# Eight weight tiles of the second feed-forward stage: sign times coefficient on ScalarE, base matrix added by a transfer

## The chip, the cores and the metric

One core of a Trainium2 chip runs the whole program in one launch. The metric is the device time of one execution in microseconds. Before the change it is 2108.03 us, the median of three runs (2106.72 to 2109.63).

## The reference

A decoder block is computed for 2 x 512 tokens of width 1024, in fp32. It has three parts, each of them behind a layer norm and added to the residual `x`: a Mamba2 layer with its own gated MLP, a quantized attention-like product with a context, and a second gated feed-forward stage whose weights are "binary differences":

```python
def _binary_diff_weight(w, base):
    d = w - base
    coeff = jnp.mean(jnp.abs(d))
    return base + coeff * jnp.sign(d)

W1, W2, W3 = (_binary_diff_weight(w, mean_w) ...)      # 3584 x 1024 each
gate = jnp.einsum('bsh,ih->bsi', hidden_states, W1)
up   = jnp.einsum('bsh,ih->bsi', hidden_states, W3)
h = jax.nn.silu(gate) * up
return jnp.einsum('bsi,hi->bsh', h, W2)
```

The coefficient is a mean over a whole matrix, so no weight of the second stage can be formed before all of `w` and `base` has been read. The first stage of the kernel reads them in passing, keeps `sign(w - base)` as int8 in DRAM (`sign_spill`) and sums the absolute differences.

## The kernel before

**Stages.** The Mamba2 layer ends at about 445 us of the span. The first feed-forward stage (`m = 0`) runs to 1226.6 us. Then comes the context product, which has no weights of its own (1226 to 1293 us), and then the second feed-forward stage (`m = 1`) to the end.

**Products.** Each feed-forward product in fp32 is three passes over rounded high and low parts (hi x hi, hi x lo, lo x hi). `weight_hi` on ScalarE (L1360) rounds a weight tile of 128 x 512 into one of seven slots of `ring_hi`. `weight_lo` on VectorE (L1835) subtracts and writes `ring_lo`. TensorE waits for `ring_lo`, multiplies (L1030 for pair 0, L1086 for the pairs after it, L1134 for the down product) and frees the slot. The 28 row blocks of gate and up are taken as 14 pairs. Pair 0 is 16 plain steps of 12 matmuls (`plain`). Pairs 1 to 13 go by a seven-product scheme that first adds and subtracts weight quarters in place (`weight_sum`, L1812 to L1820).

**Forming a weight.** `form_weight(f)` on VectorE (L2010) does `sign * coef + base` on a tile of 128 x 1024, in place in the tile that holds the base. Numbers `f` = 0 to 3 are pair 0 and stand in `raw_even`. Numbers 4 to 7 are pair 1, in `raw_odd`. SyncE loads the base tiles (`load_second`, L702) and the int8 signs (`load_sign`, L709, four buffers). Of these, 0 and 1 are formed in the middle of the context product, 2 and 3 a little later, and 4 to 7 at steps 7 to 10 of the second stage.

**Order of the work.** There is no scheduler: each engine runs its list in the order in which it is written, and waits on semaphores stand between. Around the change the order is as follows.
- SyncE loads all 16 tiles of `q2` (the quantized context, L690), waits for TensorE's last product of the first stage, and loads base and sign tiles for pair 0. Later it stores the residual tiles (`x2_spill`, L728), and then loads pair 1 and its signs.
- VectorE ends the norm of the context product with `ctx_rsqrt(2)` and starts `ctx_round(0, range(0, 2))` (L2416, L2419). Then it adds the last down product to the residual (`down_out`, L1978), and goes on rounding.
- ScalarE's part of the rounding is a Relu (L1674) and the conversion to bf16 (L1677), element tile by element tile, between two VectorE steps.
- TensorE sums the columns of `q2` (L1153), waits for `down_out`, takes the mean of the residual (L1207, L1210), and runs the context product (`ctx_first`, L1167 and L1179).
- GpSimd issues the accumulating transfers that add the per-token means to `x2_spill` (L839, 16 of 256 KB), when the context product is over.

Of the kernel before, what the change touches and what calls it, by code (L numbers as in the profile page):

```python
# [157 lines left out]
N_FORM = len(FORM_NO)  # L158

# [28 lines left out]
def build(nc, x_t, ctx, w_mamba, w_dt, w_gu, w_dn, f_gu, f_dn, b_gu, b_dn, params, shapes_only,  # L188
# [243 lines left out]
    s_hs, s_hfree = sem("hs_ready"), sem("h_region_free")  # L432
# [14 lines left out]
    s_m1, s_m2, s_x2a = (sem(n) for n in ("first_mean_kept", "second_mean", "x2_mean_added"))  # L447
# [13 lines left out]
    s_sign, s_form = sem("sign_ready"), sem("second_formed")  # L461
    s_so = [sem(f"sign_stored{i}") for i in range(2)]
# [48 lines left out]
    def value_of(m, name):  # L511
        if name in ("b11", "t2"):
            return VA[m]
        return TLf[m][{"b21": 6, "t4": 6, "b22": 5, "b12": 4, "t3": 4, "t1": 3}[name]]

# [4 lines left out]
    def _(sp):  # L520
# [95 lines left out]
        def down_loads(m):  # L616

            if m == 0:
                sp.wait_ge(s_cd, CF_BLOCKS)
            else:  # L620
                sp.wait_ge(s_wlo, gw(1, PAIRS - 1, 6, 1) + 1)
                sp.wait_ge(s_x2a, 32 * KT)
# [65 lines left out]
        for i in range(CTX_TILES):  # L688
            sp.wait_ge(s_q2o, 16 * (i + 1))
            sp.dma_start(q2[:, i, :], q2_spill[i]).then_inc(s_q2[i // KT], 16)  # L690

        def load_second(p, x):
            if p > 2:
                sp.wait_ge(s_wlo, gw(1, p - 2, 6, x) + 1)
            elif p == 2:
                sp.wait_ge(s_wlo, fw(1, 7, x) + 1)
            elif p == 1:
                sp.wait_ge(s_tv, ALL_MADE[1])
                sp.wait_ge(s_x2, 32 * KT)
            else:  # L700
                sp.wait_ge(s_pd, W_END[0])
            sp.dma_start(rawF[p % 2][:, x, :, :], b_gu[p, x].rearrange("p (j h) -> p j h", j=4)).then_inc(s_rc[p % 2][x], 16)  # L702

        def load_sign(f):
            if f >= 4:
                sp.wait_ge(s_form, f - 3)
# [25 lines left out]
        load_second(1, 0)  # L732
        load_second(1, 1)
        for f in range(4, 8):
            load_sign(f)
# [26 lines left out]
    def _(pool):  # L762
# [19 lines left out]
        pool.wait_ge(s_hfree, 1)  # L782
# [16 lines left out]

        def store_down(f):  # L800
            pool.wait_ge(s_form, f + 1)
# [7 lines left out]
        for m in range(2):  # L809
# [23 lines left out]
            if m == 0:  # L833

                pool.wait_ge(s_x2, 32 * KT)
                for b in range(BATCH):
                    pool.wait_ge(s_m2, b + 1)
                    for o in range(KT):
                        pool.dma_start(x2_spill[o][:, HALF[b]], scr_c(7)[:, HALF[b]], accum_op=ALU.add).then_inc(s_x2a, 16)  # L839
# [435 lines left out]
    def _(act):  # L1275
# [86 lines left out]
        def inner_hi(w):  # L1362
# [25 lines left out]
            else:  # L1388
# [8 lines left out]
                if m == 1 and slot >= 5:  # L1397
                    act.wait_ge(s_form, N_FORM)
# [17 lines left out]
        def move_b22():  # L1416
            act.wait_ge(s_x2a, 32 * KT)
# [76 lines left out]

        def feed_forward(m):
            part_hi_of(m, "b12")
            for w in range(BASE_G[m], W_END[m]):
# [9 lines left out]
                if m == 0 and i - 1 in CTX_AT:  # L1507
                    q2_sum(CTX_AT[i - 1])
                if 1 <= i <= NP:
# [188 lines left out]
        ctx_round(0, range(KT + 2))  # L1698
# [32 lines left out]
    def _(dve):  # L1731
# [52 lines left out]
        def raw_in(m, p, x, j):  # L1784

            if m == 1:
                dve.wait_ge(s_form, FORM_NO["g", p, x, j // 2] + 1)
# [208 lines left out]
        def form_tile(f):  # L1996
            what = FORM_WHAT[f]
            if what[0] == "d":
                return stage_d[what[1] % 2][:, :]
            return rawF[what[1] % 2][:, what[2], 2 * what[3]:2 * what[3] + 2, :].rearrange("p a h -> p (a h)")  # L2000

        def form_weight(f):
# [4 lines left out]
            else:  # L2007
                dve.wait_ge(s_rc[what[1] % 2][what[2]], 16 * (PAIRS // 2 + what[1] // 2 + 1))
# [3 lines left out]
        def feed_forward(m):  # L2012
            make(m, "b12")
            for w in range(BASE_G[m], W_END[m]):
# [29 lines left out]
                if m == 1 and i in FORM_AT:  # L2044
# [231 lines left out]
        for q in range(NC):  # L2276
# [48 lines left out]
            elif h == BATCH - 1:  # L2325
                dve.sem_inc(s_hfree, 1)
# [131 lines left out]
        form_weight(0)  # L2458
        form_weight(1)
# [10 lines left out]
        form_weight(2)  # L2470
        form_weight(3)
# [80 lines left out]
```

## Time and profile before

| | |
|---|---|
| time, median of 3 runs | 2108.03 us (2106.72 to 2109.63) |
| span of the profiled execution, first to last instruction | 2105.5 us |
| TensorE busy | 2078.2 us (99%) |
| VectorE busy | 1679.2 us (80%) |
| ScalarE busy | 1056.9 us (50%) |
| chain that ended last | PE 87%, DVE 9%, ACT 2% |

The profile gives the profiled execution's span and no time of its own beside it. The median is 2.5 us above that span. PE is TensorE, PEld its weight loads, DVE VectorE, ACT ScalarE, POOL GpSimd, SP SyncE. A row in square brackets at the end of a timeline line tells how long the engine sat idle before it, and what released it. PEclk is the granted TensorE clock as a share of 2.4 GHz.

### The profile page before, as it was taken

How to read it: one execution, taken by the hardware profiler on the slowest of the kernel's cores; microseconds unless marked ns; L12 is line 12 of the kernel's file. 1: busy time of each engine (PE TensorE's matmuls, PEld its weight loads, DVE VectorE, ACT ScalarE, POOL GpSimd, SP SyncE). 2: the span in 40 equal slices, each digit the busy share in tenths (PEclk: the TensorE clock that was granted, in tenths of full speed). 3: DMA queues.
4: the chain of work that ended last, by engine and by line, in shares of the span. 5: the costliest groups of instructions: out<-in, count | busy, mean ns of one | idle time of the engine just before them, and what ended most of it. 6: DMA issues, size and time to landing. Idle time of an engine off the chain costs nothing.

```text
span 2105.5 us, 26520 instructions
## 1 busy us (share of the span) xinstructions
PE 2078.2 (99%) x9230; PEld 1669.2 (79%) x9234; DVE 1679.2 (80%) x2528; ACT 1056.9 (50%) x1748; POOL 185.3 (9%) x296
## 2 busy tenths in 40 slices
PE   8999999999999999999999999999999999999999
PEld 4777778788888888888888845788888888888887
DVE  8888686797777888888979899977677776698886
ACT  5333244457777787774444476533333333444442
POOL 0001101101111112110000002010000000100000
PEclk9999999999999999999999999999999999999999
DMA  3151116639889999896430045454444443846101
GB/s 136 40 203 57 51 61 200 145 117 325 292 294 339 325 349 346 294 347 255 148 133 1 1 180 123 163 197 145 174 146 174 159 150 123 323 175 205 55 21 60
DMA packets 136434, 370.07 MB, mean 176 GB/s; under 512 B 16688, under 2 KB 27568, under 8 KB 132656
## 3 DMA queue, kind: packets, MB, share of 16 engines
q1 hardware_dynamic: 110640, 287.12, 39.6%
q0 software_dynamic: 25088, 80.23, 11.3%
q8 instruction: 74, 1.21, 0.2%
q10 hardware_dynamic: 576, 1.05, 0.1%
q14 instruction: 56, 0.46, 0.1%
HBM read 288.12 MB, written 84.41 MB: 177 GB/s over the span
## 4 chain that ended last, share of the span: by engine, by line
PE 87%; DVE 9%; ACT 2%; issue 1%; DMA 1%; ACTq 0%; SPq 0%; DVEq 0%
PE pair L1086 47%; PE pair L1134 24%; PE pair L856 7%; PE pair L1030 2%; DVE conv_out L2172 2%; PE pair L849 1%; PE pair L1096 1%; DVE weights_lo L1737 1%; PE pair L968 1%; PE pair L989 1%; DMA sign_in_ab<-sign_spill 1%; PE pair L1167 1%; PE pair L995 0%; DVE centred L2383 0%; DVE hs L2091 0%
## 5 line engine op out<-in xcount | busy, mean ns | idle before, releaser
L1086 PE MATMUL pair<-comb_hi,ring_hi 128*128 128x512 f32 x1456 | 566.5, 389 | 0.0
L1086 PE MATMUL pair<-comb_lo,ring_hi 128*128 128x512 f32 x1456 | 566.4, 389 | 0.0
L1086 PE MATMUL pair<-comb_hi,ring_lo 128*128 128x512 f32 x1456 | 566.4, 389 | 0.0
L1134 PE MATMUL pair<-inner_ring_a,ring_hi 128*128 128x512 f32 x1080 | 332.5, 389 | 0.0
L1086 PEld LDWEIGHTS pair<-comb_hi,ring_hi 128*128 128x128 f32 x1456 | 273.3, 188 | 57.2 <-issue 0.4
L1086 PEld LDWEIGHTS pair<-comb_hi,ring_lo 128*128 128x128 f32 x1456 | 273.3, 188 | 56.7
L1086 PEld LDWEIGHTS pair<-comb_lo,ring_hi 128*128 128x128 f32 x1456 | 273.3, 188 | 56.6
L1134 PEld LDWEIGHTS pair<-inner_ring_a,ring_hi 128*128 128x128 f32 x1080 | 202.6, 188 | 42.0
L1134 PE MATMUL pair<-inner_ring_a,ring_lo 128*128 128x512 f32 x540 | 210.1, 389 | 0.0
L1360 ACT ACTIVATE ring_hi<-ring_sum 128x512 fp32r<-128x512 f32 x160 | 100.5, 631 | 147.8 <-DVE ring_sum L1820 145.7
L1835 DVE TENSOR_TENSOR ring_lo<-raw_a,ring_hi 128x512 fp32r<-128x512 f32 x146 | 99.6, 688 | 53.4 <-ACT ring_hi L1360 51.6
L1134 PE MATMUL pair<-inner_ring_b,ring_hi 128*128 128x512 f32 x432 | 133.4, 390 | 0.0
L1134 PEld LDWEIGHTS pair<-inner_ring_a,ring_lo 128*128 128x128 f32 x540 | 101.3, 188 | 21.1
L1835 DVE TENSOR_TENSOR ring_lo<-ring_sum,ring_hi 128x512 fp32r<-128x512 f32 x160 | 109.7, 686 | 9.9 <-ACT ring_hi L1360 7.8
L856 PE MATMUL pair<-act_hi,weights_hi 128*128 128x512 f32 x256 | 108.5, 424 | 1.7 <-DVE act_lo L2274 1.4
L1986 DVE TENSOR_TENSOR pair<-coeff_in 128x1024 f32<-128x1024 f32 x84 | 103.1, 1227 | 0.0
L856 PE MATMUL pair<-act_hi,weights_lo 128*128 128x512 f32 x256 | 99.9, 390 | 0.0
L856 PE MATMUL pair<-act_lo,weights_hi 128*128 128x512 f32 x256 | 99.8, 390 | 0.0
L1486 ACT ACTIVATE sign_out<-pair 128x1024 int8<-128x1024 f32 x84 | 85.2, 1014 | 23.8 <-DVE pair L1986 23.8
L1134 PEld LDWEIGHTS pair<-inner_ring_b,ring_hi 128*128 128x128 f32 x432 | 81.1, 188 | 17.3 <-issue 0.5
L1360 ACT ACTIVATE ring_hi<-comb_hi_f 128x512 fp32r<-128x512 f32 x72 | 45.3, 630 | 94.6 <-PE pair L1134 48.5
L1360 ACT ACTIVATE ring_hi<-raw_a 128x512 fp32r<-128x512 f32 x146 | 87.4, 624 | 10.6 <-DVE raw_a L1815 7.0
(397 smaller groups left out, 3610.0 us busy)
## 6 DMA issues: line engine op xcount, KB each, us to landing
coeff_in<-f_gu SPq DMA_DIRECT2D x56, 512.0 KB, 5.3
coeff_in<-b_gu SPq DMA_DIRECT2D x56, 512.0 KB, 6.9
weights_raw<-w_mamba SPq DMA_DIRECT2D x44, 512.0 KB, 3.5
raw_a<-w_gu SPq DMA_DIRECT2D x28, 512.0 KB, 6.3
raw_a<-w_gu SPq DMA_DIRECT2D x56, 256.0 KB, 6.2
u_spill<-gate_a POOLq DMA_DIRECT2D x56, 256.0 KB, 4.9
coeff_in<-f_dn SPq DMA_DIRECT2D x28, 512.0 KB, 4.7
coeff_in<-b_dn SPq DMA_DIRECT2D x28, 512.0 KB, 6.6
```

The lines of the kernel that those rows point to most:

```text
L849: ins = pe.matmul(out[:, HALF[half]], w[:, wi, k * P:(k + 1) * P], a(half, k), start=k == 0 and n == 0, stop=k == KT - 1 and n == 2)
L856: ins = pe.matmul(out, w[:, wi, k * P:(k + 1) * P], a(b, k), start=k == 0 and n == 0, stop=k == KT - 1 and n == 2, skip_group_check=True)
L968: pe.matmul(ps[2][:, g * 512:(g + 1) * 512], bx_cur[:, 2 + g, :], xbc[:, 4 + g * HPG:4 + (g + 1) * HPG, b * SEQ + c * P:b * SEQ + (c + 1) ...
L989: ins = pe.matmul(ps[2][:, hd * P:(hd + 1) * P], x_dt[:, hd, :], att[:, hd, :], start=True, stop=c == 0)
L1030: ins = pe.matmul(out, wt[:, slot, col], a, start=j % 2 == 0 and kk == 0 and n == 0, stop=j % 2 == 1 and kk == KH - 1 and n == 2, skip_gro ...
L1086: ins = pe.matmul(out, wt[:, slot, col], a, start=t in (0, 1, 3) and kk == 0 and n == 0, stop=kk == KH - 1 and n == 2, skip_group_check=True)
L1134: ins = pe.matmul(out, wt[:, slot, col], a, start=t in (0, 1, 3) and k == 0 and n == 0, stop=k == SC_PAIRS - 1 and n == 2, skip_group_chec ...
L1360: act.activation(WRH[:, slot, :], src, ACT.Copy).then_inc(s_whi, 1)
L1486: act.activation(sign_out[:, c % 2, :], dif_ps[:, :], ACT.Sign).then_inc(s_sign, 1)
L1835: TT(WRL[:, slot, :], src, WRH[:, slot, :].bitcast(F32), ALU.subtract).then_inc(s_wlo, 1)
L1986: TT(dif_ps[:, :], dif[:, c % 2, 0, :], dif[:, c % 2, 1, :], ALU.subtract).then_inc(s_cd, 1)
L2172: ins = STT(tile[:, :, back:], src[:, :, :SEQ - back], conv_par[:, s, TAPS - 1 - back:TAPS - back], tile[:, :, back:], ALU.mult, ALU.add)
```

## The change

The weights with `f` = 0 to 7 are no longer formed on VectorE. ScalarE writes `sign * coef` into the place of the weight (`scale_sign`), and GpSimd then issues a transfer that adds the base matrix from DRAM into that place (`add_base`). SyncE no longer loads the base of pairs 0 and 1. The weights from `f` = 8 on are formed as before. One semaphore, `s_added`, now counts the base adds and the mean adds of `x2_spill` together.

```diff
+SCALED = 8
+SCALE_AT = {5: 4, 6: 5, 7: 6, 8: 7}
+ADDED = (16 * 4, 16 * (SCALED + BATCH * KT))
+MEANS_ADDED = 16 * (4 + BATCH * KT)
...
@@ sync
+        load_q2(0)
...
         for i in range(2):
             sp.wait_ge(s_so[i], 16 * (CF_BLOCKS // 2))
-        load_second(0, 0)
+        sp.wait_ge(s_pd, W_END[0])
         for f in range(4):
             load_sign(f)
-        load_second(0, 1)
+        load_q2(1)
+        for f in range(4, 8):
+            load_sign(f)
         load_down(0)
         load_down(1)
...
         spill_x2(1)
-        load_second(1, 0)
-        load_second(1, 1)
-        for f in range(4, 8):
-            load_sign(f)
@@ gpsimd
-        pool.wait_ge(s_hfree, 1)
+        pool.wait_ge(s_yt, NC + 1)
...
+        def add_base(f):
+            pool.wait_ge(s_scaled, f + 1)
+            _, p, x, h = FORM_WHAT[f]
+            pool.dma_start(form_tile(f), b_gu[p, x, :, h * BLK:(h + 1) * BLK], accum_op=ALU.add).then_inc(s_added, 16)
...
             if m == 0:
+                for f in range(4):
+                    add_base(f)
+                pool.wait_ge(s_added, ADDED[0])
                 pool.wait_ge(s_x2, 32 * KT)
...
+                pool.wait_ge(s_added, MEANS_ADDED)
+                for f in range(4, SCALED):
+                    add_base(f)
@@ scalar and vector, raw_in
-            if m == 1:
-                act.wait_ge(s_form, FORM_NO["g", p, x, j // 2] + 1)
+            if m == 1 and p < 2:
+                act.wait_ge(s_added, ADDED[p])
+            elif m == 1:
+                act.wait_ge(s_form, FORM_NO["g", p, x, j // 2] - SCALED + 1)
@@ scalar
+        def scale_sign(f):
+            act.wait_ge(s_sgn[f % 4], 16 * (f // 4 + 1))
+            if f == 0:
+                act.wait_ge(s_mc, 1)
+                act.wait_ge(s_pd, W_END[0])
+            elif f == 4:
+                act.wait_ge(s_tv, ALL_MADE[1])
+                act.wait_ge(s_x2, 32 * KT)
+            kind = FORM_WHAT[f][2]
+            act.activation(form_tile(f), sign_in[f % 4], ACT.Copy, scale=coef[:, kind:kind + 1]).then_inc(s_scaled, 1)
...
         ctx_root(2, bank(1))
-        ctx_round(0, range(KT + 2))
+        for f in range(2):
+            scale_sign(f)
+        ctx_round(0, range(2))
+        scale_sign(2)
+        ctx_round(0, range(2, KT + 2))
+        scale_sign(3)
         centred_squares(1)
@@ vector
-        form_weight(0)
-        form_weight(1)
...
-        form_weight(2)
-        form_weight(3)
...
-                if m == 1 and i in FORM_AT:
+                if m == 1 and i in FORM_AT and FORM_AT[i] >= SCALED:
                     form_weight(FORM_AT[i])
```

On ScalarE, where the context product starts (L1668 and L1704 are the end of `ctx_root(2)`, L1674 and L1710 the Relu of the rounding, L1677 and L1713 the conversion), the order before is:

```order
845 L1668 ACTIVATE scratch_c_166<-scratch_c_166 128x512
846 L1674 ACTIVATE scratch_c_165<-scratch_c_165,params 128x512 x3
847 L1677 ACTIVATE q_0_162<-scratch_c_165,quant_columns 128x512
848 L1674 ACTIVATE scratch_c_165<-scratch_c_165,params 128x512
849 L1677 ACTIVATE q_0_162<-scratch_c_165,quant_columns 128x512
```

and in the changed kernel:

```order
845 L1704 ACTIVATE scratch_c_166<-scratch_c_166 128x512
846 L1527 ACTIVATE raw_even<-sign_in_ab,coeff 128x1024 x2
847 L1710 ACTIVATE scratch_c_165<-scratch_c_165,params 128x512 x2
848 L1527 ACTIVATE raw_even<-sign_in_cd,coeff 128x1024
849 L1710 ACTIVATE scratch_c_165<-scratch_c_165,params 128x512
850 L1713 ACTIVATE q_0_162<-scratch_c_165,quant_columns 128x512
```

Two sign tiles now stand ahead of the first Relu, and a third ahead of the third Relu.

SyncE's transfers between the two feed-forward stages (`q` is `q2`, `x_spill` is `x2_spill`) are, before:

```order
335 L690 DMA q_164<-q_spill 128x1024 x16
336 L702 DMA raw_even<-b_gu 128x2048
337 L709 DMA sign_in_ab<-sign_spill 128x1024 x2
338 L709 DMA sign_in_cd<-sign_spill 128x1024 x2
339 L702 DMA raw_even<-b_gu 128x2048
340 L714 DMA down_formed_a<-b_dn 128x1024
341 L714 DMA down_formed_b<-b_dn 128x1024
342 L728 DMA x_spill<-centred 128x512 x16
343 L702 DMA raw_odd<-b_gu 128x2048 x2
344 L709 DMA sign_in_ab<-sign_spill 128x1024 x2
345 L709 DMA sign_in_cd<-sign_spill 128x1024 x2
```

and in the changed kernel:

```order
335 L704 DMA q_164<-q_spill 128x1024 x8
336 L722 DMA sign_in_ab<-sign_spill 128x1024 x2
337 L722 DMA sign_in_cd<-sign_spill 128x1024 x2
338 L704 DMA q_164<-q_spill 128x1024 x8
339 L722 DMA sign_in_ab<-sign_spill 128x1024 x2
340 L722 DMA sign_in_cd<-sign_spill 128x1024 x2
341 L727 DMA down_formed_a<-b_dn 128x1024
342 L727 DMA down_formed_b<-b_dn 128x1024
343 L743 DMA x_spill<-centred 128x512 x16
```

The first signs are now the first transfers behind the wait for the last product, the second half of `q2` stands behind them, and the signs of pair 1 are issued ahead of the residual tiles.

GpSimd's transfers around the end of the context product are, before:

```order
149 L794 DMA u_spill<-gate_a 128x512 x3
150 L839 DMA x_spill<-scratch_c_166 128x512 x16
151 L794 DMA u_spill<-gate_b 128x512 x4
152 L803 DMA wd_spill<-down_formed_a 128x1024
153 L794 DMA u_spill<-gate_b 128x512 x2
```

and in the changed kernel:

```order
149 L805 DMA u_spill<-gate_a 128x512 x3
150 L814 DMA raw_even<-b_gu 128x1024 x4
151 L857 DMA x_spill<-scratch_c_166 128x512 x16
152 L814 DMA raw_odd<-b_gu 128x1024 x4
153 L805 DMA u_spill<-gate_b 128x512 x4
```

Four base adds stand ahead of the 16 mean adds and four behind them; between the groups GpSimd waits until the earlier ones have landed.

## Rows read from the trace of the kernel before

**Rows 1.** The page: busy time and share by engine.

```profile
PE 2078.2 (99%) x9230; PEld 1669.2 (79%) x9234; DVE 1679.2 (80%) x2528; ACT 1056.9 (50%) x1748; POOL 185.3 (9%) x296
```

**Rows 2.** Stretches: length, busy of PE, PEld, DVE, ACT, POOL; clock, DMA share, GB/s.

```profile
1245.00:1294.00 49.00, 44.55 (x170) 17.55 (x171) 43.59 (x70) 38.58 (x65) 0.00 (x0) 1.00 0.23 86
1294.00:1340.00 46.00, 44.10 (x190) 34.95 (x189) 44.27 (x69) 24.73 (x44) 15.31 (x18) 1.00 0.82 194
1340.00:2050.00 710.00, 710.00 (x3133) 587.63 (x3132) 548.67 (x813) 284.23 (x485) 44.24 (x82) 1.00 0.44 157
```

**Rows 3.** Chain that ended last: start, length, what ran.

```profile
1227.16 0.73 ACT scratch_c L1674
...
1227.92 0.07 DVE scratch_c L2419
...
1228.26 2.47 DVE x_mid L1978 x4
...
1249.11 0.69 ACT scratch_c L1667
```

**Rows 4.** SyncE's timeline: start, length of the issue, transfer.

```profile
1226.90 0.33 SPq L702 DMA_DIRECT2D raw_even<-b_gu  x1
1227.28 0.92 SPq L709 DMA_DIRECT2D sign_in_ab<-sign_spill  x2
```

**Rows 5.** The sign loads of 1200 to 1400 us (L709), issue to landing.

```profile
DMA to landing us min/median/max: 1.9/4.4/12.8
```

**Rows 6.** ScalarE's groups of 500 to 1100 us: busy, mean ns of one.

```profile
L1493 ACT ACTIVATE q_out<-q_out 128x1024 bf16<-128x1024 bf16 x16 | 16.8, 1053 | 5.7 <-DVE q_out L1994 5.7
```

**Rows 7.** TensorE's timeline around the start of the context product.

```profile
1226.65 1.75 PE L1153 MATMUL pair<-ones_bf,q 128*128 128x1 bf16 x64
1229.09 1.10 PE L1207 MATMUL pair<-scratch_c,ones_over_dm 128*128 128x512 f32 x2 [0.68 <-DVE x_mid L1978]
...
1233.67 0.59 PE L1167 MATMUL pair<-q,q 128*128 128x512 bf16 x2
...
1243.77 1.75 PE L1153 MATMUL pair<-ones_bf,q 128*128 128x1 bf16 x64
1245.39 3.68 PE L1161 MATMUL pair<-x_mid,ones_over_dm 128*128 128x512 f32 x8
```

**Rows 8.** TensorE's timeline near the program's start.

```profile
5.75 5.71 PE L866 MATMUL pair<-conv_out,ones_over_dm 128*128 128x512 f32 x8 [5.75 <-DVE conv_out L2086]
15.23 0.50 PE L882 MATMUL pair<-act_hi,weights_hi 128*128 128x512 f32 x1 [3.77 <-DVE act_lo L2097]
```

**Rows 9.** Stretch behind that idle time, columns as in rows 2.

```profile
16.00:21.00 5.00, 4.83 (x14) 3.34 (x14) 5.00 (x9) 4.00 (x7) 0.00 (x0) 0.66 0.70 271
```

**Rows 10.** VectorE's timeline, weights 0 and 1, and 4.

```profile
1247.46 2.48 DVE L2010 SCALAR_TENSOR_TENSOR raw_even<-sign_in_ab,coeff,raw_even 128x1024 f32<-128x1024 int8 x2
1250.48 0.69 DVE L2406 SCALAR_TENSOR_TENSOR scratch_c<-scratch_c 128x512 f32<-128x512 f32 x1 [0.54 <-ACT scratch_c L1668]
...
1326.51 1.28 DVE L2010 SCALAR_TENSOR_TENSOR raw_odd<-sign_in_ab,coeff,raw_odd 128x1024 f32<-128x1024 int8 x1 [1.24 <-DMA sign_in_ab<-sign_spill]
```

**Rows 11.** TensorE's timeline, the waits at the end of pair 0.

```profile
1333.26 0.50 PE L1030 MATMUL pair<-comb_hi,ring_hi 128*128 128x512 f32 x1 [0.29 <-DVE ring_lo L1835]
1337.47 0.50 PE L1030 MATMUL pair<-comb_hi,ring_hi 128*128 128x512 f32 x1 [1.19 <-DVE ring_lo L1835]
1340.33 0.39 PE L1086 MATMUL pair<-comb_hi,ring_hi 128*128 128x512 f32 x1
```

**Rows 12.** Stretch within the mean adds, columns as in rows 2.

```profile
1300.00:1306.00 6.00, 5.68 (x23) 4.25 (x24) 5.81 (x11) 3.52 (x7) 6.00 (x10) 1.00 1.13 196
```

**Rows 13.** The 16 mean adds (L839): first and last start, issue to landing.

```profile
L839 POOL DMA_DIRECT2D x_spill<-scratch_c x16: 884/3406/6030, 1294.5 to 1302.7; - x16
...
DMA to landing us min/median/max: 3.8/10.9/22.4
```

**Rows 14.** ScalarE's timeline at weight 16, the first of pair 1.

```profile
1327.83 0.63 ACT L1360 ACTIVATE ring_hi<-raw_odd 128x512 fp32r<-128x512 f32 x1 [6.16 <-DVE raw_odd L2010]
```

More of the change, by code:

```diff
@@ L446, in build @@
     s_g, s_mc = sem("q2_row_summed"), sem("mean_constants_ready")
-    s_m1, s_m2, s_x2a = (sem(n) for n in ("first_mean_kept", "second_mean", "x2_mean_added"))
+    s_m1, s_m2, s_added = (sem(n) for n in ("first_mean_kept", "second_mean", "bases_and_x2_means_added"))
     s_col, s_row, s_xo, s_xt = sem("column_sums"), sem("row_sums"), sem("ctx_product"), sem("ctx_taken")
@@ L514, in value_of, with form_tile @@
         return TLf[m][{"b21": 6, "t4": 6, "b22": 5, "b12": 4, "t3": 4, "t1": 3}[name]]
+    def form_tile(f):
+        what = FORM_WHAT[f]
+        if what[0] == "d":
+            return stage_d[what[1] % 2][:, :]
+        return rawF[what[1] % 2][:, what[2], 2 * what[3]:2 * what[3] + 2, :].rearrange("p a h -> p (a h)")
     PLAIN_BANK = {0: (4, 5), 2: (0, 2), 1: (1, 3), 3: (6, 7)}
@@ L687, in _, with load_q2 @@
         sp.wait_ge(s_ulo, ND)
-        for i in range(CTX_TILES):
-            sp.wait_ge(s_q2o, 16 * (i + 1))
-            sp.dma_start(q2[:, i, :], q2_spill[i]).then_inc(s_q2[i // KT], 16)
+        def load_q2(b):
+            for i in range(b * KT, (b + 1) * KT):
+                sp.wait_ge(s_q2o, 16 * (i + 1))
+                sp.dma_start(q2[:, i, :], q2_spill[i]).then_inc(s_q2[b], 16)
+        load_q2(0)
         def load_second(p, x):
@@ L694, in load_second @@
                 sp.wait_ge(s_wlo, gw(1, p - 2, 6, x) + 1)
-            elif p == 2:
+            else:
                 sp.wait_ge(s_wlo, fw(1, 7, x) + 1)
[L697 to L701, printed above, removed]
             sp.dma_start(rawF[p % 2][:, x, :, :], b_gu[p, x].rearrange("p (j h) -> p j h", j=4)).then_inc(s_rc[p % 2][x], 16)
         def load_sign(f):
-            if f >= 4:
-                sp.wait_ge(s_form, f - 3)
+            if f >= SCALED + 4:
+                sp.wait_ge(s_form, f - SCALED - 3)
+            elif f >= 4:
+                sp.wait_ge(s_scaled, f - 3)
             what = FORM_WHAT[f]
@@ L1508, in feed_forward @@
                     q2_sum(CTX_AT[i - 1])
+                if m == 1 and i in SCALE_AT:
+                    scale_sign(SCALE_AT[i])
                 if 1 <= i <= NP:
@@ L1784, in raw_in @@
         def raw_in(m, p, x, j):
-            if m == 1:
-                dve.wait_ge(s_form, FORM_NO["g", p, x, j // 2] + 1)
+            if m == 1 and p < 2:
+                dve.wait_ge(s_added, ADDED[p])
+            elif m == 1:
+                dve.wait_ge(s_form, FORM_NO["g", p, x, j // 2] - SCALED + 1)
             elif j < 2:
```

22 lines of the change are left out of this document (8 added, 14 removed).

## The prediction

> **What bounds the kernel now.** I read the page first: TensorE is busy for 99% of the span [rows 1], so only a stretch in which it waits can give or cost time. The stretches come next [rows 2]. In the second feed-forward stage from 1340 to 2050 us TensorE is busy for all of 710 us, with VectorE busy for 549. Whatever VectorE saves there is worth nothing, and a delay made earlier is carried through unchanged. TensorE's idle time near the change lies in the context product (4.4 of 49 us) and in pair 0 behind it (1.9 of 46 us). The third view is the chain of waits, which names the engine that binds inside the context product. At its start the chain goes from ScalarE's first Relu to VectorE's clamp and then to `down_out` [rows 3]. TensorE stands behind `down_out`: it has been idle for 0.68 us when L1207 starts [rows 7]. So in this place ScalarE binds, although it is the engine with half its time free.
>
> **Part 1: two scalings ahead of the first Relu (a cost).** `scale_sign(0)` waits for its sign tile, whose load waits for the last product of the first stage. SyncE was released at 1226.90 [rows 4], and in the changed order the signs are the first transfers there. A load of 128 KB has landed 1.9 us after its issue at best, 4.4 in the middle of a stretch with other traffic [rows 5]. Before, a 1 MB base load went first; now the queue is empty, so I take 2.1 us, near the lower end: the sign is there at 1229.0. Scaling 128 x 1024 is not in the trace; the nearest row is L1493, a copy of the same size with a sum, at 1.05 us [rows 6]. Consecutive instructions overlap a little, so two take about 1.95 us. The first Relu then starts at 1230.95, not at 1227.16 [rows 3]: 3.8 us late. With a landing after 1.9 us and nothing else changed it would be 3.6, after 4.4 us 6.1.
>
> Is anything else there to absorb it? VectorE is in order and waits for this Relu before its clamp, and `down_out` stands behind the clamp [rows 3]. TensorE's L1207 needs the first tile of `down_out`. The rest of the context product hangs on these three, link by link, so I let all of the 3.8 us through. The third scaling falls into the time in which VectorE does the 2.47 us of `down_out` [rows 3] and ScalarE has nothing: free. The fourth stands behind the last conversion and ahead of `centred_squares(1)`; ScalarE follows VectorE's subtractions there and catches up, so I count 0, at most 1.0.
>
> **Part 2: the half clock (a cost that hangs on part 1).** TensorE ends the column sums at 1228.4 (1226.65 plus 1.75) and started L1207 at 1229.09 [rows 7]. That start moves to 1232.9, so TensorE idles 4.5 us instead of 0.7, right behind 64 matmuls of one column. Near the start of the program it idled for 3.77 us before 15.23 [rows 8], and the granted clock then was 0.66 over the five microseconds from 16 [rows 9], a mix of 1.0 and 0.5: 5 x 0.34 = 1.7 us of TensorE time lost. If this happens here, it hits L1207, the mean (to 1233.67) and the first matmuls of `ctx_first`, after which TensorE runs without a gap to the end of L1161 at 1249.07 [rows 7]. ScalarE's next root starts at 1249.11 [rows 3]: no slack, so the loss counts in full. The bounds are 0 and about 2.5 us; I take 1.7, from the only such place in the trace.
>
> The Trainium skill ("TensorE: Matmul & The Clock Gate", the section "Part 1: The HAM clock gate") says that idle time closes the gate to half the rate and that sustained work opens it again. The trace agrees at 16 us; by the page the longer gap here would do the same.
>
> **Part 3: VectorE's eight forms go (a gain where they bind).** A form takes 1.28 us, about 1.2 in a row [rows 10]. Forms 0 and 1 are followed by 0.54 us in which VectorE waits for ScalarE [rows 10]: nothing gained. Forms 2 and 3 lie beside TensorE's context matmuls: nothing gained. Forms 4 to 7 stand in pair 0, where VectorE has 44.3 of 46 us busy [rows 2]. There it also waits 1.24 us for a sign tile [rows 10]. TensorE waits 0.29 and 1.19 us for `ring_lo` [rows 11], together 1.48. VectorE reaches the last of these 1.24 + 3 x 1.2 = 4.8 us sooner, more than the wait. So 1.48 us is gained. No more is to be had: behind it TensorE never waits [rows 2].
>
> ScalarE pays for it with four scalings of about 1 us at steps 5 to 8. Before it reaches weight 16 it sat idle for 6.16 us [rows 14], which covers them.
>
> **Part 4: the base adds (cost nothing if they land in time).** The first four are 512 KB each. Tile 3 is scaled when the rounding of the first half is done, and the tiles are wanted only at the end of the rounding of the second half, so these adds are hidden. The second four wait for the 16 mean adds. An add into SBUF is not in the trace. The nearest row is the mean adds themselves, into DRAM, during which the DMA engines were full and moved 196 GB/s [rows 12]. 4.19 MB at that rate is 21.4 us from 1295.5 [rows 13], so they end near 1317. Then 2.10 MB take 10.7 us, with 3.8 us for a landing at best [rows 13]: the last base add lands near 1331. It is wanted at 1340.33 - 1.48 = 1338.9, less 1.4 us for high and low part (0.63 for the high part [rows 14] and little more for the low): 1337.5 [rows 11]. Margin 6 us; the shift moves both sides alike. At half the rate (98 GB/s) the landing is near 1342 and TensorE waits about 5 us. At twice the rate it is near 1326.
>
> The Trainium skill ("DMA: Bandwidth & Descriptors", the section "Anatomy of one DMA — SWDGE (gpsimd) path") fits such a transfer as 2.0 us plus bytes over 436e3. The estimate from this page is 3.2 us for each base add, and earlier landings than mine. The trace's 196 GB/s for adds speaks against it. The sum would be the same, but the chance of late adds would be smaller.
>
> GpSimd holds the stores of pair 0's inner values behind these adds, some 10 us later than before. Nobody reads them until the down product. The second half of `q2` is issued behind the signs, and TensorE wants it at 1243.77 [rows 7] plus 3.8; 2 MB and three base adds are done some 4 us before. The replaced wait on GpSimd in the Mamba2 part is released at the same instruction: 0.
>
> **Sum.** +3.8 (Relu) +1.7 (clock) -1.5 (pair 0) = +4.0 us on a span of 2105.5, so 2109.5. The median of the runs is 2.5 us above the span, and the change leaves that part alone: 2112.0 us.
>
> **The rivals.**
> - *The clock stays up.* +3.8 - 1.5 = +2.3 us: 2110.3. For it: the 4.4 us of idle time spread over 1245 to 1294 left the clock at 1.00 [rows 2], and one precedent is thin. Against it: the gap here is longer than the one that cost the clock.
> - *The base adds come late.* Something like half the rate: +4.0 + 4.5 = 2116.5 us. TensorE would wait at the first step of pair 1. For it: the load of pair 2's base falls in the same time. Against it: 6 us of margin.
> - *VectorE binds after all (faster).* In 1245 to 1340 VectorE is busy for 88 of 95 us [rows 2], more than the chain's view of single links tells. If its forms counted in full, 8 x 1.2 = 9.6 us and 1.24 of waiting would go and 3.8 come: -7.0, or 2101.0. It decides from the point where more than 3.8 us is saved, where I count 1.48. Against it: VectorE's own 0.54 us of waiting behind forms 0 and 1.
> - *The shift is absorbed,* because the last down product or the mean waits for something that I have not seen. Then only -1.5 or 0 remains: 2107 to 2108.
>
> **How the numbers follow.** The forecast with the clock lost has 0.50, the clock kept 0.27, late adds 0.12, VectorE binding 0.05, absorption 0.06. What a measurement of this kernel can tell from no change is 0.2%, 4.2 us: below 2103.8 is faster, above 2112.2 slower. The forecast, with about 1.3 us of spread, splits nearly in halves at the upper border: 0.24 slower, 0.26 the same. The clock kept gives 0.24 the same and 0.03 slower. Late adds are slower, absorption is the same, VectorE binding mostly faster. Together: faster 0.06, same 0.55, slower 0.39. The range is 2108.0 to 2116.5. It takes in landings of the sign up to 4.4 us and the lower part of the late adds.
>
> **What would show it.** Right: a first Relu about 3.8 us later counted from the last product; a gap of 4 to 5 us in TensorE before the mean's matmul; PEclk below 1.0 there; no wait on `ring_lo` at steps 14 and 15; the last base add landed before ScalarE's high part of weight 16 is needed. Wrong: a Relu at its old distance (part 1), the full clock (part 2), waits of TensorE for pair 1 (part 4), or a context product that is no longer than before from the last product to L1030.

## The result and the profile after

| | before | after |
|---|---|---|
| median | 2108.38 us (6 runs, 2106.68 to 2109.77) | 2117.41 us (6 runs, 2113.22 to 2117.78) |
| profiled execution | span 2105.5 | 2117.15, span 2115.2 |
| ratio after / before | | 1.0036, 95% interval 1.0026 to 1.0046 |

The changed kernel is slower by 5.5 to 9.7 us with 95% confidence, 7.6 us at the middle. The forecast was +4.0 us, 2112.0, with a range up to 2116.5. By the ratio the changed kernel stands at 2115.6 against the 2108.03 of before, within the range; the median of its six runs lies 0.9 us above the range's upper end. Two executions, one of e3 (5453 us) and one of e4 (3530 us), ran far longer than all others and enter no median, mean or ratio here. The sign and the main mechanism came out, the size did not; the forecast's chances had 0.55 for a change within its 4.2 us and 0.39 for slower. The page's line on the engines, against [rows 1]:

```profile
PE 2083.7 (99%) x9230; PEld 1671.7 (79%) x9234; DVE 1670.2 (79%) x2520; ACT 1065.0 (50%) x1756; POOL 191.6 (9%) x304
```

VectorE gave up 9 us of work and ScalarE took 8 over; the span grew by 9.7. TensorE's own landmarks cut the two profiled executions into five stretches, which the sections below take one by one:

| stretch on TensorE | before | after | difference | forecast |
|---|---|---|---|---|
| start to the column sums behind the last product | 1226.65 | 1229.04 | +2.39 | 0 |
| column sums to the first context matmul | 7.02 | 13.37 | +6.35 | +5.5 |
| from there to pair 0 | 59.79 | 59.79 | 0.00 | 0 |
| pair 0 | 46.87 | 45.38 | -1.49 | -1.48 |
| pair 1 to the end | 765.17 | 767.62 | +2.45 | 0 |

Second stretch first, since the forecast put its weight there. ScalarE's timeline of the changed kernel:

```profile
1225.92 0.63 ACT L1704 ACTIVATE scratch_c<-scratch_c 128x512 f32<-128x512 f32 x1
1231.39 1.15 ACT L1527 ACTIVATE raw_even<-sign_in_ab,coeff 128x1024 f32<-128x1024 int8 x1 [4.84 <-DMA sign_in_ab<-sign_spill]
1233.17 1.15 ACT L1527 ACTIVATE raw_even<-sign_in_ab,coeff 128x1024 f32<-128x1024 int8 x1 [0.63 <-DMA sign_in_ab<-sign_spill]
1234.23 1.32 ACT L1710 ACTIVATE scratch_c<-scratch_c,params 128x512 f32<-128x512 f32 x2
```

L1527 is the new scaling and L1710 the first Relu. ScalarE stands idle for 4.84 us before sign 0 and for 0.63 us more before sign 1. The chain of waits passes through the second of these:

```profile
1229.29 0.32 SPq L722
1229.65 3.50 DMA sign_in_ab<-sign_spill
1233.17 1.15 ACT raw_even L1527
1234.32 0.62 ACT scratch_c L1710
1235.03 0.35 issue
1235.38 0.68 DVE x_mid L2021
1236.19 2.04 PE pair L1228 x2
```

Sign 0 was scaled from 1231.39 on, 2.10 us after its issue at 1229.29, which is the landing that the forecast took. Sign 1, a load of 128 KB with only sign 0's ahead of it, took 3.50 us, and it is the one that the chain passes through. The Relu starts 5.19 us behind the column sums instead of 0.51 [rows 3, 7]: 4.68 late. TensorE's timeline answers to [rows 7]:

```profile
1229.04 1.75 PE L1174 MATMUL pair<-ones_bf,q 128*128 128x1 bf16 x64
1236.19 2.04 PE L1228 MATMUL pair<-scratch_c,ones_over_dm 128*128 128x512 f32 x2 [5.40 <-DVE x_mid L2021]
1238.03 4.33 PE L1231 MATMUL pair<-x_mid,ones_over_dm 128*128 128x512 f32 x8
1242.41 0.59 PE L1188 MATMUL pair<-q,q 128*128 128x512 bf16 x2
```

The gap is 5.40 us instead of 0.68. From the mean's first matmul to the first context matmul it takes 6.22 us instead of 4.58, so 1.64 us more at an unchanged instruction count: 4.71 + 1.64 = 6.35. The stretches show why, a clock of 0.50, the lower of the two levels (1.2 GHz) (columns: window, length, PE busy, granted clock, DMA share, GB/s):

```profile
1232.00:1234.00 2.00, 0.00 (x0) 0.67 0.76 206
1234.00:1236.00 2.00, 0.00 (x0) 0.50 0.90 225
1236.00:1238.00 2.00, 1.81 (x2) 0.50 0.95 192
1238.00:1240.00 2.00, 2.00 (x4) 0.63 1.04 224
```

Pair 1: GpSimd's timeline, and then the landing times of all eight base adds (L814).

```profile
1303.29 14.19 POOL L857 DMA_DIRECT2D x_spill<-scratch_c  x16 [53.89 <-DVE scratch_c L2470]
1329.99 3.54 POOL L814 DMA_DIRECT2D raw_odd<-b_gu  x4 [12.51 <-DMA x_spill<-scratch_c]
```

```profile
DMA to landing us min/median/max: 6.3/9.4/14.4
```

The mean adds run from 1303.29 to 1329.99, 26.7 us, and the four base adds of pair 1 behind them reach ScalarE only at 1346.17. The two engines that split the weight, and TensorE behind them:

```profile
1346.17 0.63 ACT L1383 ACTIVATE ring_hi<-raw_odd 128x512 fp32r<-128x512 f32 x1 [11.60 <-DMA raw_odd<-b_gu]
```

```profile
1346.83 0.69 DVE L1878 TENSOR_TENSOR ring_lo<-raw_odd,ring_hi 128x512 fp32r<-128x512 f32 x1 [5.61 <-ACT ring_hi L1383]
1350.06 0.69 DVE L1878 TENSOR_TENSOR ring_lo<-raw_odd,ring_hi 128x512 fp32r<-128x512 f32 x1 [1.33 <-ACT ring_hi L1383]
```

```profile
1347.58 0.50 PE L1107 MATMUL pair<-comb_hi,ring_hi 128*128 128x512 f32 x1 [0.46 <-DVE ring_lo L1878]
1350.81 0.50 PE L1107 MATMUL pair<-comb_hi,ring_hi 128*128 128x512 f32 x1 [0.17 <-DVE ring_lo L1878]
```

Two more waits, of 0.73 and 0.38 us, follow at 1360 and 1372. The stretch from pair 1 to the end grew by 2.45 us. Of pair 0's two waits [rows 11] none is left, but the 0.46 us in front of pair 1's first matmul lies inside the 45.38 us of the table's row for pair 0.

The first stretch, +2.39 us, lies 900 us ahead of the work that the change is about. VectorE's and GpSimd's timelines of the kernel before show how the reload of the residual was released:

```profile
324.08 2.16 DVE L2312 SCALAR_TENSOR_TENSOR conv_out<-conv_out,params,pair 128x128 f32<-128x128 f32 x8
335.25 0.69 DVE L2359 TENSOR_TENSOR h_residual<-h_residual,pair 128x512 f32<-128x512 f32 x1 [1.45 <-DMA h_residual<-hs_spill]
```

```profile
324.42 1.85 POOL L785 DMA_DIRECT2D h_residual<-hs_spill  x2 [27.83 <-DVEq L2326]
```

and those of the changed kernel:

```profile
324.61 2.16 DVE L2349 SCALAR_TENSOR_TENSOR conv_out<-conv_out,params,pair 128x128 f32<-128x128 f32 x8
338.21 0.69 DVE L2394 TENSOR_TENSOR h_residual<-h_residual,pair 128x512 f32<-128x512 f32 x1 [3.88 <-DMA h_residual<-hs_spill]
```

```profile
327.06 1.85 POOL L796 DMA_DIRECT2D h_residual<-hs_spill  x2 [29.95 <-DVE conv_out L2349]
```

Before, the increment was an instruction of its own behind the eight STTs. An STT is one SCALAR_TENSOR_TENSOR instruction. The reload started at 324.42, released by VectorE's sequencer (`DVEq`), when the STTs had just begun. The new wait counts what the last STT signals when it ends, at 326.8. So the reload starts about 2.1 us later against the work around it, and VectorE waits 3.88 us for it instead of 1.45. TensorE gets a wait that it did not have:

```profile
341.83 0.50 PE L877 MATMUL pair<-act_hi,weights_hi 128*128 128x512 f32 x1 [0.52 <-DVE weights_lo L1778]
```

Three parts make up the 2.39 us, read off as how much later the same VectorE instruction starts. At the STTs it is 0.53 us (324.61 against 324.08); the granted clock was lower from 10 to 25 us (0.77 against 0.89), and no run shows why. Over the reload it grows by 0.78. The other 1.07 come between 700 and 830 us, where TensorE has its only wait from 420 us to the column sums:

```profile
805.04 0.47 PE L1107 MATMUL pair<-comb_hi,ring_hi 128*128 128x512 f32 x1 [0.49 <-ACT gate_a L1461]
```

### The profile page after: what moved, and what is told of

It is laid out like the page before. It is cut to its first block, busy times and chain, and to the rows that moved or that the text cites. A ratio compares the mean times of both kernels' runs of the same rounds, so it can differ in the third digit from the quotient of the medians.

```text
span 2115.2 us, 26516 instructions
## 1 busy us (share of the span) xinstructions
PE 2083.7 (99%) x9230; PEld 1671.7 (79%) x9234; DVE 1670.2 (79%) x2520; ACT 1065.0 (50%) x1756; POOL 191.6 (9%) x304
## 3 DMA queue, kind: packets, MB, share of 16 engines
q10 hardware_dynamic: 576, 1.05, 0.1%
## 4 chain that ended last, share of the span: by engine, by line
PE 86%; DVE 7%; DMA 3%; ACT 2%; issue 1%; POOL 0%; ACTq 0%; DVEq 0%; SPq 0%; POOLq 0%
PE pair L1107 45%; PE pair L1155 24%; PE pair L877 6%; PE pair L1051 2%; DVE conv_out L2209 2%; PE pair L870 1%; PE pair L1117 1%; PE pair L903 1%; PE pair L1188 1%; DMA x_spill<-scratch_c 1%; DVE weights_lo L1778 1%; DMA raw_odd<-b_gu 1%; PE pair L989 1%; PE pair L1010 1%; DMA h_residual<-hs_spill 1%
```

## The experiments

A bold name is a kernel. "Relu" and "mean" are their starts behind the column sums. Ratios are to the kernel before, run on the same chip. Means are over the runs that enter the ratio. The changed kernel's is 2116.3, over the six runs of the result; it was not run again beside the experiments, and the kernel before has 2108.6, 2108.3 and 2108.0 beside e1 to e4, e5 to e8 and e9 to e12. A difference of under 1 us to the changed kernel is therefore not shown by the means.

**1. Both scalings behind the first Relus (e1).**

```
-for f in range(2): scale_sign(f)
 ctx_round(0, range(2))
-scale_sign(2)
+for f in range(2): scale_sign(f)
 ctx_round(0, range(2, KT + 2))
+scale_sign(2)
 scale_sign(3)
```

> The changed kernel with the scalings of tiles 0 and 1 behind the first two Relus instead of ahead of them, and 2 and 3 behind the last conversion. Theory (the two scalings ahead of the Relu hold VectorE's down_out and so TensorE): the first Relu is back at 0.5 us after the last product, TensorE's idle time before the mean's matmul is back at 0.7 us, PEclk stays 1.00 there, and the time falls by 4.7 + 1.6 us, less up to 0.7 us because tile 1's sign may land after the third Relu is due: about 5.7 us below the changed kernel, 1 to 2 us above the kernel before (ratio 1.0005 to 1.001). Rival (the shift comes from the transfers beside it: base adds and the late second half of q2): the stretch from the last product to the first conversion product stays 3 us or more longer than before.

2111.03 us (10 runs), ratio 1.0010, 1.0001 to 1.0020; mean 5.2 us under the changed kernel. Relu +0.53, mean +2.45, TensorE's gap 0.69. So the place of two 1.15 us instructions, with the wait in front of them, costs most of the loss. But the clock fell all the same:

```profile
1230.00:1232.00 2.00, 1.30 (x37) 1.00 0.73 182
1232.00:1234.00 2.00, 2.00 (x4) 0.60 0.75 221
1234.00:1236.00 2.00, 2.00 (x4) 0.55 0.93 234
1236.00:1238.00 2.00, 2.00 (x7) 1.00 0.85 170
```

That is half clock behind an idle time of 0.69 us. The late adds stayed too (from pair 1 on, 767.09 us).

**2. Only the wait (e2).** As e1, with the first Relu waiting for sign 1 and no scaling ahead of it:

```
+act.wait_ge(s_sgn[1], 16)
 ctx_round(0, range(2))
```

> The same as e1_behind_relus, but ScalarE still waits for tile 1's sign to land before the first Relu; only the work of the two scalings is moved behind. It parts waiting from work. Theory (most of the 4.7 us is the wait for a transfer that can't start before the last product): Relu 2 to 3.5 us later than before, idle time of TensorE about 3 to 4 us, the half clock in some runs; 2.5 to 5 us over the kernel before. Rival (the work of two scalings, 2.2 us, is what counts): within 1 us of e1_behind_relus.

2115.68 us, ratio 1.0035, 1.0021 to 1.0049. Relu +4.27: 3.76 of the 4.68 us are waiting for the signs, and the other 0.92 is about one scaling, since the other one runs while sign 1 is on its way. ScalarE's row:

```profile
1233.01 1.33 ACT L1710 ACTIVATE scratch_c<-scratch_c,params 128x512 f32<-128x512 f32 x2 [6.75 <-DMA sign_in_ab<-sign_spill]
```

**3. TensorE kept at work in the gap (e3).** The changed kernel with 20 matmuls whose result nobody reads:

```
 column_sums(0, bank(3))
+pe.wait_ge(s_mc, 1)
+for _ in range(20):
+    pe.matmul(bank(2), ones_bf[:, :], q2[:, 0, 0:H], start=True, stop=True)
```

> The changed kernel with 20 matmuls of 512 columns (bf16, result not used) put into TensorE's gap behind the column sums of q2: 4.3 us of work in a gap of 5.4. ScalarE and VectorE are as in the changed kernel, so the Relu and down_out stay late by 4.7 us. Theory (the gap makes the granted clock fall to half, which costs 1.6 us): PEclk 1.00 from 1226 to 1245, the stretch from the start of the mean's matmul to the first context matmul is 4.6 us as before and not 6.2, and the time is 1.6 us below the changed kernel where that one lost its clock. Rival (the clock falls for another reason, or the matmuls are slow because of the DMA traffic): PEclk below 1.00 again and no gain.

2115.50 us (5 runs), ratio 1.0033, 1.0020 to 1.0047. The stretches, the two of interest first:

```profile
1232.00:1236.00 4.00, 3.54 (x17) 1.00 0.77 216
1236.00:1240.00 4.00, 3.11 (x8) 1.00 0.86 163
...
1295.00:1300.00 5.00, 5.00 (x8) 0.69 0.15 55
```

The clock stayed up where it fell before. From the mean's first matmul to the second group of column sums it took 14.68 us, as in the kernel before, instead of 16.32. In the same trace the clock then fell 60 us further on, behind a wait of 2.03 us that every trace has there, and that stretch grew by 1.60 us. So this trace gained next to nothing in all, and the mean of the runs, 0.8 us lower, shows no gain either.

**4. Pair 1 formed by VectorE, with its signs loaded early (e4).** `SCALED = 4`, the base loads of pair 1 back on SyncE behind x2's stores, no base adds behind the mean adds.

> The changed kernel with only the first four weights on ScalarE and adds; weights 4 to 7 are formed on VectorE as before, but their signs are loaded early, ahead of the residual tiles. Theory (the late base adds of pair 1 starve VectorE for 7 us and TensorE loses 3.1 us to it, against 1.9 before): VectorE no longer waits for anything but ScalarE in pairs 0 and 1, ring_lo of steps 14 and 15 comes 1.2 us sooner than before, TensorE's waits in pairs 0 and 1 fall under 1 us, and the time is about 2 us below the changed kernel (the Relu part stays: 4.5 to 5 us over before). Rival (the excess of pair 1 is from ScalarE's four scalings): it falls too, so the trace decides: with the theory VectorE's idle time of 5.6 us before weight 16 is gone and its forms take its place without a wait of TensorE.

2114.80 us (8 runs), ratio 1.0030, 1.0020 to 1.0041; mean 1.5 us under the changed kernel. From pair 1 to the end 765.14 us, the kernel before's value (765.17): the tail cost is gone. This edit takes away the four adds and the four scalings together; e5 keeps the scalings.

**5. Half of the mean adds left out (e5).** The output lacks the mean on half of x2's rows, and the counts that are waited for are lower to match.

```
-for o in range(KT):
+for o in range(KH):
     pool.dma_start(x2_spill[o]..., accum_op=ALU.add).then_inc(s_added, 16)
```

> The changed kernel with 8 of the 16 mean adds into x2_spill left out (half of the feature rows don't get their mean). Theory (the base adds of pair 1 are late because they stand behind 16 mean adds, which take 25 to 27 us): the mean adds are done about 12 us sooner, the base adds of pair 1 are bound by ScalarE's last scaling (some 28 us after the first plain product) and land some 5 us before the last mean add would allow, ScalarE's idle time before weight 16 falls from 11.6 to under 5 us, VectorE's 5.6 us of waiting before it to under 1, and the stretch from the first plain product to the first Silu of pair 1 falls from 65.4 to about 62.5 to 63 us: 2 to 3 us of time. Rival (ScalarE's scalings or the store traffic are the cause): that stretch stays above 64.5.

2113.47 us (8 runs), ratio 1.0024, 1.0014 to 1.0035; mean 2.7 us under the changed kernel, and 764.87 us from pair 1 on. GpSimd's timeline shows base adds that wait for their scaling and no longer for mean adds:

```profile
1302.85 7.09 POOL L857 DMA_DIRECT2D x_spill<-scratch_c  x8 [53.95 <-DVE scratch_c L2470]
1324.30 0.87 POOL L814 DMA_DIRECT2D raw_odd<-b_gu  x1 [14.36 <-ACT raw_odd L1527]
```

ScalarE reaches weight 16 at 1340.34, 5.8 us sooner, and 5.4 us sooner counted from the start of pair 0. With e4, two removals of different parts say the same: the late adds are the cause of the tail. The base adds are now bound by their scalings; the last starts at 1331.28, and TensorE has no wait for them.

**6. The kernel before with signs 4 to 7 loaded ahead of x2's second store (e6).** It moves four loads and nothing else, and aims at the 1.24 us wait of [rows 10]; e12 is the same kernel once more.

```
 spill_x2(0)
+for f in range(4, 8): load_sign(f)
 spill_x2(1)
 load_second(1, 0)
 load_second(1, 1)
-for f in range(4, 8): load_sign(f)
```

> The kernel before with one edit: the signs of weights 4 to 7 are loaded between the two halves of the residual's stores, ahead of pair 1's bases, so that they don't land last. Theory (of pair 0's 1.48 us of waiting for ring_lo, 1.24 come from the wait for the sign): VectorE's 1.24 us are gone, TensorE's waits at steps 14 and 15 fall from 1.48 to under 0.5, and the time is 1 to 1.3 us below the kernel before, ratio 0.9995. Rival (VectorE then waits as long for the base tile, whose load is under way in the same time): VectorE waits for raw_odd and no time is gained.

> The kernel before with nothing but the signs of forms 4 to 7 loaded ahead of x2's stores, once more, beside the kernel it is compared with: it was 1.3 us under the kernel before with an interval that reached 1. 'VectorE's wait for a sign is worth its length': 1.0 to 1.5 us under the kernel before, 2107.1, TensorE's wait near 1337 is 0.4 us. 'It is only odds': within 0.5 us of the kernel before.

2106.89 us (11 runs), ratio 0.9993, 0.9984 to 1.0002, and the second time 2108.11 (11 runs), 0.9999, 0.9990 to 1.0009. In both traces TensorE's two waits of 1.48 us [rows 11] have become one, here e12's:

```profile
1336.16 0.50 PE L1030 MATMUL pair<-comb_hi,ring_hi 128*128 128x512 f32 x1 [0.41 <-DVE ring_lo L1835]
```

In the traces pair 0 is 1.33 and 1.36 us shorter; the times of 22 runs do not settle it (means 1.2 and 0.3 us under the kernel before). Of e12's runs 5 took 2106.1 to 2106.9 and 6 took 2108.1 to 2109.5, and the latter had the lower mean clock (0.997 to 0.998 against 0.999). Such a step of about 2 us outweighs the gain.

**7. Four forms on ScalarE, spread out (e7).** e4 with the scalings between ScalarE's conversions and none ahead of a Relu. e11 adds the early release of the reload.

```
-for f in range(2): scale_sign(f)
 ctx_round(0, range(2))
-scale_sign(2)
+scale_sign(0)
 ctx_round(0, range(2, KT + 2))
-scale_sign(3)
+scale_sign(1)
 ...
 ctx_round(1, range(0, 2))
+scale_sign(2); scale_sign(3)
 ctx_round(1, range(2, 4))
```

> Four weights on ScalarE with base adds, the scalings where ScalarE waits anyway: tile 0 behind the first two Relus, tile 1 behind the last conversion of the first half, tiles 2 and 3 behind the first two Relus of the second half; weights 4 to 7 on VectorE with early signs. Theory (VectorE's forms 0 to 3 cost nothing in the kernel before, and ScalarE's wait was the whole price of moving them): the context product is as long as before within 0.5 us, pair 0 is as in e6_before_early_signs, so the time equals that of e6 within 1 us and is 0 to 1.5 us below the kernel before. Rival (VectorE's forms in the context product cost something): it is 1 to 2.5 us below e6.

> The kernel with only forms 0 to 3 on ScalarE, their scalings spread between ScalarE's conversions (none ahead of the first Relu), pair 1 formed by VectorE with its signs loaded early, and the reload released early as in the kernel before. It took 2109.2 with the late reload. 'Late reload': 2106.8, 1.6 below the kernel before and level with the kernel before with early signs, which says that VectorE's four forms ahead of pair 0 cost nothing where they stood. 'VectorE's forms bind there': below 2105.5, more than 1.3 us under the kernel before with early signs. 'Chance': 2109.

e7: 2108.85 us (11 runs), ratio 1.0004, 0.9995 to 1.0013. e11: 2106.75 us (11 runs), ratio 0.9996, 0.9987 to 1.0005. e11 is level with e6 and e12 within 1 us, and its pair 0 is as long as theirs (45.55 against 45.51 and 45.54 us), so VectorE's forms 0 to 3 cost nothing there that could be measured. It is the best version of the idea, and it cannot be told from the kernel before.

**8. The kernel before, profiled again (e8).** No edit.

> The kernel before, unchanged, for one more trace: is the granted clock at the column sums (1226 to 1245 us) always 1.00 in it? If TensorE's short gap of 0.7 us there is safe, it is 1.00 again. If not, half clock shows up in this place without the change too, as it did in e1_behind_relus with a gap of 0.69, and the 1.6 us of the clock are a matter of odds and not a part of the change alone.

2108.07 us in one run. Same landmarks to 0.1 us up to the context product (column sums at 1226.61, Relu +0.50, context +7.00). Its clock then fell in a later place, behind the wait of 2.03 us that e3 lost its clock at:

```profile
1285.00:1290.00 5.00, 2.97 (x5) 0.66 0.28 105
```

**9. Only the replaced wait (e9, e10).** e9 is the kernel before with the changed kernel's wait; e10 is the changed kernel with the early release (counted on `s_scaled`, whose later counts are one higher).

```
-pool.wait_ge(s_hfree, 1)
+pool.wait_ge(s_yt, NC + 1)
```

> The kernel before with one edit: GpSimd releases the reload of the residual in the Mamba2 part when VectorE's last STT there has ended (the changed kernel's wait), not when its sequencer passes the increment behind it. In the profile of before the reload starts at 324.42 beside those STTs (324.08 to 326.24); in that of the changed kernel it starts at 327.06 behind them, and VectorE waits 3.88 us for it where it waited 1.45. Theory 'late reload': VectorE's idle time before its first residual add is 3.9 to 4.3 us, the last product of the first feed-forward stage ends 2.2 to 2.6 us later than in the kernel before (column sums start near 1229.0, not 1226.6), and the kernel takes 2.4 us more, about 2110.8 against 2108.4. Theory 'chance' (the later start of the column sums comes from clock losses early in the program, or from where the code lies): the column sums start near 1226.6 and the time is within 0.5 us of the kernel before.

> The changed kernel with the reverse edit: the reload of the residual is released by an increment in VectorE's instruction stream again, as in the kernel before (counted on the semaphore of the scalings, since no other is left; all its later counts are one higher). The rest of the change stays. 'Late reload': the column sums start near 1226.7, the rest of the stage is as in the changed kernel (Relu 5.2 us and first matmul of the mean 7.2 us behind them), and the kernel takes 2.4 us less than the changed one, about 2113.9 against 2116.3, a ratio to before near 1.0026. 'Chance': about 2116, the column sums at 1228 to 1229.5.

e9: 2110.77 us (11 runs), ratio 1.0013, 1.0004 to 1.0022, 2.7 us above the kernel before's median; the lowest run is 2108.80 against 2106.61. Its timelines of VectorE and TensorE:

```profile
338.53 0.69 DVE L2359 TENSOR_TENSOR h_residual<-h_residual,pair 128x512 f32<-128x512 f32 x1 [4.40 <-DMA h_residual<-hs_spill]
```

```profile
342.15 0.50 PE L856 MATMUL pair<-act_hi,weights_hi 128*128 128x512 f32 x1 [1.04 <-DVE weights_lo L1737]
```

What the late reload costs can be read in every trace, from the STTs to the addition of the residual that follows near 419 us, here before and in e9:

```profile
418.82 0.68 DVE L2359 TENSOR_TENSOR h_residual<-h_residual,pair 128x512 f32<-128x512 f32 x1
420.45 0.68 DVE L2359 TENSOR_TENSOR h_residual<-h_residual,pair 128x512 f32<-128x512 f32 x1
```

It takes 94.67 to 94.74 us in the six traces with the early release (before, e6, e8, e10, e11, e12) and 95.52 to 96.02 in the eight with the late one. So 0.8 to 1.3 us of the cost is this wait: 0.78 in the changed kernel, 1.27 in e9. e9's column sums start 3.06 us later than the kernel before's; another 1.42 belong to one wait of TensorE for ScalarE at 691.29. Such a wait, at 691, 727 or 805 us, stands in traces with either release (e6 and e11 have it with the early one, the changed kernel with the late one) and is missing in others, so it isn't shown to be the change's. By the means the late release costs 2.9 us here and 1.6 us between e11 and e7, each against the kernel before on its chip; what they have above 1.3 stays open.

e10 took 2116.37 us (5 runs), ratio 1.0037, 1.0024 to 1.0051: the 2.4 us did not come back. In its trace the release did what it should (the reload starts beside the STTs, and from there to the residual it takes 94.70 us). But this trace was 0.92 us later than the changed kernel's already at the STTs, and it lost more to the clock afterwards:

```profile
1230.00:1235.00 5.00, 0.00 (x0) 0.54 0.74 219
1235.00:1240.00 5.00, 4.80 (x6) 0.50 0.98 222
1240.00:1245.00 5.00, 5.00 (x16) 0.94 1.07 246
```

From the mean's first matmul to the second column sums it took 17.36 us there, 1.04 more. Whether that is chance, 5 runs do not say. So the times show the cost of the replaced wait in the kernel before (e9), and in the changed kernel only the traces do.

## Why the prediction was right, and where its sizes were off

The forecast's direction and its main term held. The ratio puts the cost at 7.6 us, 3.6 above the forecast and near the upper end of the range. That the total stayed inside it owes something to luck: two costs counted as nothing (the late adds and the replaced wait) came on top, and one gain was larger than counted.

- *Part 1, Relu 3.8 us late: right, mis-sized.* It was 4.68. The landing of 2.1 us was right for sign 0; the term that was too small is sign 1's, which the sum has no landing for and which needed 3.50. The scalings cost less than counted (1.95), because the first one runs in the wait for sign 1. All of it passed on to TensorE, as said; the idle time there grew by 4.72. e1 and e2 confirm it from both sides. The third and the fourth scaling cost 0.00 us up to pair 0.
- *Part 2, half clock +1.7: size right, reason half right.* It cost 1.64 us, and in e3's trace work in the gap kept the clock up there. But a short gap is no protection. With 5.38 to 5.93 us of idle time, or 4.44 in e2, the clock fell in 5 of 5 traces. With 0.7 us it fell at this place in 4 of 8 (e1, e6, e7, e9), for 1.70 us each (16.38 instead of 14.68 us from the mean's first matmul to the second column sums). So a loss that came in half of these traces came in all five with the long gap. The cost is 1.7 us against the one profile that had kept its clock, and by these traces about half of that (an estimate) against the mean of many runs. The Trainium skill ("TensorE: Matmul & The Clock Gate", "Part 1: The HAM clock gate") puts the half rate down to idle time; e1, with 0.69 us of it, shows that the length of the gap alone does not decide here.
- *Part 3, -1.48 in pair 0: right in kind, and its exact size is luck.* The profiled trace has -1.49, but it holds the 0.46 us wait for the late weight 16. In e1, e2, e5 and e10, which have no such wait there, pair 0 takes 44.77 to 44.83 us instead of 46.87: -2.1. The idle times of [rows 11] add up to less than the waits cost. In e6 and e12 the early signs alone gave 1.33 to 1.36 of it with VectorE still forming all eight weights, so most of what bound there was the sign's landing; the other 0.7 us came with VectorE's forms 4 to 7 (e4, which keeps them, has 45.57). Four forms fewer ahead of pair 0 gave nothing more (e7, e11).
- *Part 4, base adds on time: wrong.* A margin of 6 us stood against 5.3 us more for the mean adds (26.7, not 21.4) and 1.7 more for the base adds (16.2, not 14.5). The rate of 196 GB/s came from the middle of the mean adds and is that of all transfers of the stretch together; 4.19 MB in 26.7 us is 157 GB/s. They begin slowly, before as well (53 GB/s from 1294.5 to 1297) and here:

```profile
1303.00:1306.00 3.00, 3.00 (x15) 1.00 0.46 62
1306.00:1310.00 4.00, 3.60 (x15) 1.00 1.12 151
1310.00:1318.00 8.00, 7.98 (x35) 1.00 1.09 187
1318.00:1326.00 8.00, 8.00 (x37) 1.00 1.13 206
```

  A whole batch of transfers is priced from its first start to its last landing, which [rows 13] already held: 1294.5 to 1302.7 for the starts, and up to 22.4 us for one landing. (The prediction starts its 21.4 us at 1295.5, which no row has.) That landing is of one of the last eight adds, which started from 1298.9 on, so the mean adds ended at 1321 or later and not near 1317. The prediction also left out that a base add waits for its scaling, the last at step 8 of pair 0: the last base add starts at 1331.28 in e5, where the mean adds no longer hold it. This was the rival with a chance of 0.12; it came in mildly, +2.45 instead of +4.5, on top of the forecast. And 2.45 is the largest of five traces: e10, e1, e3 and e2 have 2.14, 1.92, 1.05 and 0.80. By the fit of the Trainium skill ("DMA: Bandwidth & Descriptors", "Anatomy of one DMA — SWDGE (gpsimd) path") the estimate for one such add is 3.2 us; the landings took 6.3 to 14.4.
- *The replaced wait "released at the same instruction: 0": wrong.* It is the same place in the code, but one counts when the sequencer passes, the other when the work has ended, and it cost 0.8 us in this trace. The prediction read the diff and not the row of the reload (above), which names `DVEq` as its releaser.
- *The rivals.* VectorE binding in the context product is refuted by e11; in pair 0 its forms were worth the 0.7 us above, not 9.6. Absorption did not happen: from the first context matmul to pair 0 both traces take 59.79 us.

The sum after the fact, on the profiled executions: +4.7 (gap), +1.6 (clock), -1.5 (pair 0), +2.45 (late adds), +2.4 (ahead of the stage) = +9.7, with rounding. Of the 2.4 the reload's wait has 0.8, the wait for ScalarE at 805.04 has 1.1, and 0.5 is there before the reload; only the first is shown to be the change's. The ratio has +7.6 and not +9.7. That fits with clock losses and waits for ScalarE that come to the kernel before as well, and with a smaller tail in most traces, but no run parts them.

## What to carry to other kernels

Do not put work for later, however short, behind a fresh transfer on the engine that heads the chain: the transfer's landing and not the work is the price (3.8 of 4.7 us here). When a semaphore is replaced by another "at the same place", ask whether each is raised by the sequencer or by the end of the work, and look in the trace for who released the waiter. Price a queue of transfers by the whole batch, first start to last landing, and not by the rate in its middle.

## What the runs showed of the hardware

- TensorE's clock went to half behind a gap of 0.7 us that follows 64 one-column matmuls in 4 of 8 traces, each time for a loss of 1.70 us. Single executions of the kernel before lie up to 5.5 us apart (2106.19 to 2111.73 beside e1), and one profile of the kernel before does not show which part of a difference is the clock.
- An increment that stands as an instruction of its own in VectorE's stream was seen 1.8 us before the end of the arithmetic ahead of it (324.42, where the STTs end at 326.24).
- Adding transfers that queued together, beside the other traffic of the stage: 4.19 MB of adds into DRAM took 26.7 us, then 2.10 MB into SBUF 16.2 us.
- A wait of TensorE cost more than the idle time that the profile shows for it: 0.52 us at 341.83 in the changed kernel and 1.04 us at 342.15 in e9 made everything behind them 0.78 and 1.27 us later, and pair 0's 1.48 us of waits in the kernel before cost 2.1.
- ScalarE scales a 128 x 1024 int8 tile into f32 in 1.13 to 1.15 us, and two in a row in 2.17 (e7, e11).
